# Single first images on ScalarE, the value chain in parts of two and six blocks, the low passes bank by bank, and half a query inside the last product

## What is computed

```python
keys    = xf @ Wk.T                     # (32, 1024, 16)
values  = bn(xf @ Wv.T, per position)   # (32, 1024, 32)
queries = bn(xf @ Wq.T, per k)          # (32, 16, 1024, 4)
content_lambda   = einsum('bmk,bmv->bkv', softmax(keys, axis=1), values)
position_lambdas = einsum('nmk,bmv->bnkv', E, values)     # E is (1024, 1024, 16)
out = x + einsum('bknh,bkv->bhvn', queries, content_lambda)
        + einsum('bknh,bnkv->bhvn', queries, position_lambdas)
```

## Time and profile before

| | |
|---|---|
| median of three runs | 1455.75 us (1455.48 to 1455.85) |
| the profiled execution's own time | 1455.59 us |
| its span | 1453.5 us |
| PE busy | 1426.0 us (98%) |
| DVE, ACT, POOL busy | 852.9 (59%), 752.2 (52%), 421.5 us (29%) |
| mean granted TensorE clock | 0.997 |

### The profile page before, as it was taken

One profiled execution on the slowest core, in us unless ns is written; L12 is line 12 of the kernel. 1 busy time (PEld: TensorE's weight loads), 2 busy tenths in 40 slices (PEclk: granted clock), 3 DMA queues, 4 the chain that ended last, 5 costly groups with the idle time before them and its releaser, 6 DMA issues.

```text
span 1453.5 us, 36061 instructions
## 1 busy us (share of the span) xinstructions
PE 1426.0 (98%) x14551; PEld 1187.9 (82%) x14551; DVE 852.9 (59%) x1217; ACT 752.2 (52%) x1104; POOL 421.5 (29%) x360
## 2 busy tenths in 40 slices
PE   6989999999999999999999999999999999999998
PEld 6987878888888888888888888888888888888886
DVE  7998665555555555555555555555555555555553
ACT  4775465554555455455554555545555454545542
POOL 6683131233223321233223321333123322332120
PEclk9999999999999999999999999999999999999999
DMA  8744413434252333424252333425252233425221
GB/s 290 278 167 90 100 37 87 94 77 84 62 123 65 84 74 87 94 70 89 65 123 65 75 78 93 94 62 97 65 123 65 66 85 94 94 53 105 65 58 29
DMA packets 342618, 134.65 MB, mean 93 GB/s; under 512 B 206800, under 2 KB 337984, under 8 KB 342080
## 3 DMA queue, kind: packets, MB, share of 16 engines
q1 hardware_dynamic: 342592, 134.31, 38.7%
HBM read 109.12 MB, written 25.17 MB: 92 GB/s over the span
## 4 chain that ended last, share of the span: by engine, by line
PE 90%; DVE 0%; issue 0%; DVEq 0%
PE ps_a L1142 81%; PE ps_b L1158 5%; PE ps_a L1126 3%; PE ps_b L1099 0%; DVE lam_diag L864 0%; DVE pos L840 0%; DVE pos L832 0%; DVE res L850 0%; PE ps_b L1107 0%; DVEq L837 0%; DVEq L723 0%
## 5 line engine op out<-in xcount | busy, mean ns | idle before, releaser
L1142 PE MATMUL ps_a<-v_hi,e_hi 128*128 128x512 f32 x1708 | 670.4, 393 | 1.0 <-issue 1.0
L1142 PE MATMUL ps_a<-v_hi,e_lo 128*128 128x512 f32 x1708 | 664.7, 389 | 0.0
L626 ACT ACTIVATE q_diag<-q_blk,q_shift_n,q_scale_n 128x256 f32<-128x256 f32 x512 | 411.4, 868 | 43.7 <-PE ps_b L1158 41.6
L562 ACT ACTIVATE e_hi<-e_nat 128x512 fp32r<-128x512 f32 x305 | 192.8, 633 | 443.2 <-PE ps_a L1142 436.7
L1142 PE MATMUL ps_a<-b_lo,e_hi 128*128 128x512 f32 x976 | 379.6, 389 | 0.0
L1142 PEld LDWEIGHTS ps_a<-v_hi,e_hi 128*128 128x128 f32 x1708 | 320.5, 188 | 68.8 <-issue 1.4
L1142 PEld LDWEIGHTS ps_a<-v_hi,e_lo 128*128 128x128 f32 x1708 | 320.7, 188 | 64.9
L474 POOL TENSOR_TENSOR e_nat<-e_nat,s_buf 128x512 f32<-128x512 f32 x61 | 79.7, 1306 | 927.8 <-DVE e_lo L717 927.8
L807 DVE TENSOR_TENSOR pos<-ps_a,content 128x512 f32<-128x512 f32 x183 | 126.6, 692 | 295.7 <-PE ps_a L1142 295.7
L717 DVE TENSOR_TENSOR e_lo<-e_nat,e_hi 128x512 fp32r<-128x512 f32 x305 | 290.6, 953 | 3.6 <-ACT e_hi L562 3.3
L1142 PE MATMUL ps_a<-t_lo,e_hi 128*128 128x512 f32 x732 | 285.5, 390 | 0.0
(11 more groups left out here) (126 smaller groups left out, 875.8 us busy)
## 6 DMA issues: line engine op xcount, KB each, us to landing
e_nat<-in_L_conv_E SPq DMA_DIRECT2D x128, 512.0 KB, 4.9
res<-in_x SPq DMA_DIRECT2D x64, 256.0 KB, 6.0
out_dram<-res SPq DMA_DIRECT2D x60, 256.0 KB, 4.7
x_main<-in_x SPq DMA_DIRECT2D x24, 512.0 KB, 4.5
q_dram<-q_nat SPq DMA_DIRECT2D x4, 2048.0 KB, 7.6
q_blk<-q_dram SPq DMA_DIRECT2D x32, 256.0 KB, 3.0
x_more<-in_x SPq DMA_DIRECT2D x8, 512.0 KB, 8.6
out_dram<-res SPq DMA_DIRECT2D x4, 192.0 KB, 4.0
```

The costliest lines, as they stand in the source:

```text
L562: nc.scalar.activation(e_hi[:, i], e_source(i, slot), ACT.Copy).then_inc(e_hi_ready, 1)
L626: ins = nc.scalar.activation(to[:, n], of, ACT.Identity, bias=q_shift_n[:, n:n + 1], scale=q_scale_n[:, n:n + 1])
L1142: ins = nc.tensor.matmul(BANK_OF[i], e[:, i, j].rearrange("p n k -> p (n k)"), v[:, j], start=(STARTS[i] and j == 0 and n == 0), stop=(STO ...
```

## The change

- The first batches of images are now 1, 1, 2, 2, 2 images, then four each. The images of the first three batches (0 to 3) are normalised by ScalarE (norm_image) instead of GpSimd, which ends at the bias for them. VectorE's statistics of the first batches are interleaved by half images with gn_finish. TensorE projects image 1 ahead of the transposes of image 2, and averages at the places of AVERAGE_AT.
- TensorE gets dummy transposes of the identity (warm): 12 ahead of the first average, 4 and 7 after it, 30 after the last projection.
- The value chain is in parts of blocks 0 to 1 and 2 to 7 (V_PARTS); affine(0) stands behind the statistics of the second part and ahead of its aggregation. ScalarE splits block 0 in two halves, and TensorE starts with the banks of the first half. keys_max(3) stays behind affine(1).
- first_hi(0, 2) and (0, 3) on ScalarE and first_lo(2) on GpSimd come earlier. sum_keys(2) waits for key_max_ready, not for keys_shifted. e_sums of pair 3 waits for q_affine.
- The banks of the plain pairs go in the order a, c, d, b. spread_content stands ahead of the second half of the low passes, which go bank by bank; lam_scale stands between value_split_lo(4) and (6).
- add_out(2) and evacuate_u2(3) stand ahead of split_lo(3, 6) and (4, 0).
- The last pair is taken out of TensorE's loop; its last product is cut in two, with the left half of its query between them; the additions and stores of its output go by halves.

```diff
-    BATCHES = [(0, GB // 2), (GB // 2, GB // 2)] + [(b, GB) for b in range(GB, B, GB)]
+    BATCHES = [(0, 1), (1, 1), (2, 2), (4, 2), (6, 2)] + [(b, GB) for b in range(2 * GB, B, GB)]
+    ACT_NORMED, ACT_BATCHES = 4, 3
+    V_PARTS = (range(0, 2), range(2, J))
...
@@ GpSimd
+                ins = pool.tensor_tensor(gn_bias[:, sl], gn_out[:, sl, 1], gn_rstd[:, sl], ALU.mult)
+                if k < ACT_BATCHES:
+                    ins.then_inc(gn_biased, 1)
+                    return
...
             first_lo(1)
+            first_lo(2)
             sum_keys(1)
             shift_keys(2)
-            first_lo(2)
             first_lo(3)
             values_rstd(0)
             values_rstd(1)
-            pool.wait_ge(keys_shifted, A)
+            pool.wait_ge(key_max_ready, A)
             sum_keys(2)
             sum_keys(3)
             queries_rstd()
+            pool.wait_ge(q_affine, 1)
             e_sums(PLAIN, PLAIN % 2, 64, first=True)
...
@@ ScalarE
+            def norm_image(b, k):
+                act.wait_ge(gn_biased, k + 1)
+                xi = x_in(b)
+                nc.scalar.activation(xi, xi, ACT.Identity, bias=gn_bias[:, b:b + 1], scale=gn_rstd[:, b:b + 1]
+                                     ).then_inc(x_normed_act, 1)
+            norm_image(0, 0)
+            norm_image(1, 1)
...
                     read_xt(8 * a + i, i, a == 0)
+                    if (a, i) == (A - 1, G - 1):
+                        first_hi(0, 3)
+                    if (a, i) == (0, 1):
+                        norm_image(2, 2)
+                        norm_image(3, 2)
...
             act.wait_ge(v_affine, 1)
-            for j in range(MJ):
-                values_hi(j)
+            first_values_hi(0)
+            first_values_hi(1)
+            values_hi(1)
+            act.wait_ge(v_affine, 2)
+            values_hi(2)
+            values_hi(3)
             normalise(3)
             normalise(2)
             exp_keys(3)
-            act.wait_ge(v_affine, 2)
...
@@ VectorE
+            for part, js in enumerate(V_PARTS):
                 link(value_stats(A - 1, A, range(G - 2, G), js))
+                if part == 1:
+                    affine(0)
                 for j in js:
                     ins = nc.vector.bn_aggr(v_mv[:, j], v_stats[:, j].rearrange("p a s -> p (a s)"))
...
+            affine(1)
...
-            for i in (4, 6):
-                value_split_lo(i)
+            value_split_lo(4)
             lam_scale()
+            value_split_lo(6)
...
             split_lo(PLAIN, 5, PLAIN % 2)
+            add_out(PLAIN - 1, new_block=False)
+            evacuate_u2(PLAIN)
...
+            add_half(PAIRS - 1, 0)
             evacuate_c12(PAIRS - 1)
-            add_out(PAIRS - 1, new_block=False)
+            add_half(PAIRS - 1, 1)
...
@@ TensorE
+            def warm(count):
+                for n in range(count):
+                    nc.tensor.transpose(ps_a[:, 1, 0:P], ident[:], ident[:])
             pe.wait_ge(consts, 6)
+            warm(12)
...
             gn_average(0, 0)
+            pe.wait_ge(weights_loaded, 16 * 3)
+            nc.tensor.transpose(ps_a[:, 0, 0:PC], w_rows[:], ident[0:PC, 0:PC]).then_inc(w_transposed, 1)
+            warm(4)
             pe.wait_ge(gn_read, 1)
             gn_average(1, 0)
             pe.wait_ge(w_ready, 1)
+            warm(7)
+            AVERAGE_AT = {1: 3, 3: 4}
+            for k in range(5, len(BATCHES)):
+                AVERAGE_AT[4 * (k - 5) + 5] = k
...
             project(B - 1, G - 1)
+            warm(30)
...
             for j in range(MJ):
+                if j == 0:
+                    pe.wait_ge(v_hi_first, 1)
+                    plain_sums(0, j, (0, 1), only=(0, 1))
                 pe.wait_ge(v_hi_ready, j + 1)
-                plain_sums(0, j, (0, 1))
+                plain_sums(0, j, (0, 1), only=(2, 3) if j == 0 else None)
...
-            pe.wait_ge(v_lo_ready, 4)
-            for j in range(MJ, J):
-                if j == J - 3:
-                    spread_content()
-                plain_sums(0, j, (2,), last=(j == J - 1))
+            spread_content()
+            for at in range(4):
+                pe.wait_ge(v_lo_ready, (3, 3, 4, 4)[at])
+                for j in range(MJ, J):
+                    plain_sums(0, j, (2,), last=(j == J - 1), only=(at,))
...
-            with pe.Fori(PLAIN + 1, PAIRS) as p:
+            with pe.Fori(PLAIN + 1, PAIRS - 1) as p:
                 pair(p)
-            query(PAIRS - 1)
+            product(PAIRS - 1, 0, False)
+            query(PAIRS - 2)
+            for i in range(1, NP - 1):
+                product(PAIRS - 1, i, False)
+            product(PAIRS - 1, NP - 1, False, range(0, MJ // 2))
+            query_half(PAIRS - 1, 0)
+            product(PAIRS - 1, NP - 1, False, range(MJ // 2, MJ))
+            query_half(PAIRS - 1, 1)
```

More of the change, by code:

```diff
@@ L442, in sum_keys, with values_rstd @@
                 pool.tensor_tensor(of_a, level[:, 0], level[:, 1], ALU.add).then_inc(exp_summed, 1)
-            def values_rstd(half):
-                js = slice(half * MJ, half * MJ + MJ)
-                pool.wait_ge(v_var_ready, half + 1)
+            def values_rstd(part):
+                js = slice(V_PARTS[part].start, V_PARTS[part].stop)
+                pool.wait_ge(v_var_ready, part + 1)
                 pool.tensor_tensor(v_rstd[:, js], v_var[:, js], minus_half[:, js], ALU.pow).then_inc(v_rstd_ready, 1)
@@ L760, in group @@
                 keys_max(a)
-            for k in range(4):
-                gn_moments(k)
-                gn_finish(k)
-            gn_moments(4)
+            gn_moments(0)
+            gn_moments(1, halves=range(0, 1))
+            gn_finish(0)
+            gn_moments(1, halves=range(1, 2))
+            gn_moments(2, range(0, 1), range(0, 1))
+            gn_finish(1)
+            gn_moments(2, range(0, 1), range(1, 2))
+            gn_moments(2, range(1, 2))
+            gn_moments(3, range(0, 1))
+            gn_finish(2)
+            gn_moments(3, range(1, 2))
+            gn_moments(4, range(0, 1))
+            gn_finish(3)
+            gn_moments(4, range(1, 2))
             gn_moments(5, range(0, 2))
@@ L834, in evacuate_first @@
             def evacuate_first(p):
-                for n, (bank, t, cols) in enumerate(((bank_a, 0, left), (bank_d, 1, right), (bank_c, 1, left),
+                for n, (bank, t, cols) in enumerate(((bank_a, 0, left), (bank_c, 1, left), (bank_d, 1, right),
                                                      (bank_b, 0, right))):
@@ L891, in _, with affine @@
             value_stats(A - 1, A - 1, range(G - 2))
-            for half in range(2):
-                js = range(half * MJ, half * MJ + MJ)
+            def affine(part):
+                js = slice(V_PARTS[part].start, V_PARTS[part].stop)
+                dve.wait_ge(params_loaded, 16 * (2 + 2 * TN))
+                dve.wait_ge(v_rstd_ready, part + 1)
+                link(nc.vector.tensor_tensor(v_scale[:, js], v_rstd[:, js], gam_v[:, js], ALU.mult))
+                link(nc.vector.tensor_tensor(v_tmp[:, js], v_mv[:, js, 0], v_scale[:, js], ALU.mult))
+                nc.vector.tensor_tensor(v_shift[:, js], bet_v[:, js], v_tmp[:, js], ALU.subtract).then_inc(v_affine, 1)
+            for part, js in enumerate(V_PARTS):
                 link(value_stats(A - 1, A, range(G - 2, G), js))
+                if part == 1:
+                    affine(0)
                 for j in js:
@@ L980, in pair @@
                     split_lo(p + 1, 0, (i + 1) % 2)
-                add_out(p - 1, new_block=(i == 1))
-                evacuate_u2(p)
+                if not second:
+                    add_out(p - 1, new_block=(i == 1))
+                    evacuate_u2(p)
                 if not last:
@@ L1111, in _, with plain_sums @@
             EVACUATED_BEFORE = (-1, 1, 0, 2, -2, 3, 4)
-            def plain_sums(p, j, passes, last=False):
+            def plain_sums(p, j, passes, last=False, only=None):
                 half, slots_of = j // MJ, FIRST_SLOTS[p]
-                for at, (tile, col, bank) in enumerate(((0, 0, bank_a), (1, 1, bank_d), (1, 0, bank_c), (0, 1, bank_b))):
+                for at, (tile, col, bank) in enumerate(((0, 0, bank_a), (1, 0, bank_c), (1, 1, bank_d), (0, 1, bank_b))):
+                    if only is not None and at not in only:
+                        continue
                     hi = v_hi[:, (0, 4)[half] + col, j % MJ]
@@ L1131, in plain_sums, with product @@
                 return ins
-            def product(p, i, first):
+            def product(p, i, first, js=range(MJ)):
                 pe.wait_ge(e_lo_ready, p * NP + i + 1)
@@ L1139, in product @@
                 hi, lo = value_hi(i), value_lo(i)
-                for j in range(MJ):
+                for j in js:
                     for n, (e, v) in enumerate(((e_hi, hi), (e_lo, hi), (e_hi, lo))):
```

110 lines of the change are left out of this document (70 added, 40 removed).

## The result

The changed kernel takes 1446.65 us (median of 4 runs, 1445.76 to 1447.59) where the kernel before, run beside it, takes 1455.80 (1455.48 to 1456.25): a ratio of 0.9935, 95% interval 0.9923 to 0.9948. Forecast was 1448.3, or 7.45 us less than before; measured are 9.15. Two later series, on chips 12 and 11, gave 9.13 and 8.71.

The account below looks back on a forecast made before the run. The pair loop runs without waits, so only TensorE's standstills and slow stretches elsewhere can be won: 1455.59 - 2.7 (first images) - 3.4 (handover) - 1.0 (pair 3) - 0.3 (end) = 1448.2, against the median 1448.3; range 1446.6 to 1451.2.

Parts of the forecast that it names:

- The start: First images: with one image in the first batch, transposes start earlier; -2.7 us, between -1.2 and -3.3.
- the gain is carried on: Rest of the first stage: TensorE's longest wait is 0.3 us and other engines follow its averages, so -2.7 us stays.
- The handover: From images to products: earlier turn 1.3, three waits gone 2.5, less 0.4; -3.4 us, between -1.6 and -3.9.
- The turn: turn_key_max, behind the first eight matmuls, waits for keys_max and moves from 113.45 to 112.1: -1.3 us.
- Rival 1: Clock falls again while TensorE waits 2.2 us for key_max; eight slow matmuls cost 1.6 us: 1449.9, chance 0.17.
- rival 2: Pair 2's tile load or the first diagonal query is late; only 1.3 of 3.4 us stays: 1450.4, chance 0.10.
- The three waits: TensorE's waits for the values' low part, lam_diag, and the content and first bank all go: 2.5 us, counted by starts.
- The 0.4 against sum_keys(2): Handover: sum_keys(2)'s new place holds one VectorE instruction once; spread up to 1.2 us late, 0.4 of it costing time.
- Pair 3: Fourth product's 1.00 us wait at 204.59 goes as the evacuation moves ahead: -1.0 us, or nothing if VectorE isn't free.
- The end: Last query, addition and stores: half the addition saved, perhaps some issues; -0.3 us, between +0.3 and -0.9.
- rival 5: Behind pair 3 the loop falls into another rhythm, each of 59 pairs waiting; at 0.2 us a pair 1460, chance 0.02.
- Rivals 3 and 4: ScalarE's four normalisations bound the first images, 1449.8, chance 0.07; VectorE bounds the handover, 1453.4, chance 0.03.

Follow-up runs that it names:

- the kernel with pair 3 alone: The kernel before with only add_out and evacuate_u2 of pair 3 moved ahead of the loop's three steps: median 1455.15 us, 1.25 us less, ratio 0.9992.

## Why the prediction was right or wrong

The sign, the places and their order held; the gain is 1.7 us larger than the sum. 1446.65 is just above the low end of the range, 1446.6; the ratio of 0.9935, taken of the 1455.75 on which the range stands, gives 1446.3, below it. The two later series, with 9.13 and 8.71, lie at its low end and inside it.

The 1.7 us have two parts. 0.55 come from the stages, 8.00 between the profiled executions for 7.45: less at the start (0.8), more in the handover (0.25), pair 3 (0.25), the loop (0.2) and the end with its stores (0.6). That the sum of the stages came so near is in part luck, as terms wrong by up to 0.8 us cancelled. The other 1.15, the larger part, stand in no stage. **The step that failed most is the last one of the sum:** it was made on one profiled execution and carried to the median with 0.16 us, as if both kernels' executions stood to their medians alike, and the range left no room for it. The profiled execution was 0.21 below the median in the kernel before, and 0.94 above it in the changed kernel.

**The start** was right as far as it was costed: image 0 at 9.8 (10.2 said), image 4 at 21.57 (21.6 said), -3.0 for -2.7. The step that failed here is the sentence that the gain is carried on through the rest of the stage. first_lo(2) moved ahead of sum_keys(1), and of that move I costed nothing, though I asked for the queue of every step moved. It held key_diag and gave back 1.1 us; undoing the move won it back. This made the gain smaller, not larger.

**The handover**: -3.4 said, -3.65 between the two profiled executions; the total was near, but of its parts only the turn was. The turn: I said that it moves by 1.3 us beyond the start's shift; it came 1.6 earlier against the last projections (11.34 for 12.93), because the clock stayed up and key_max was as early as said. Rival 1 was wrong: at 1.00 through the wait of 1.63 us. The first query, rival 2, was hidden with 1.4 to spare, and without the wait for q_affine TensorE waited 0.8 for it. The three waits all went; undone they cost 1.7, as much as their rows in the kernel before add up to, so my 2.5 from starts was too high for that part. 1.6 and 1.7 leave some 0.3 of the 3.65 that no experiment places. The 0.4 against sum_keys(2) was the wrong kind of term: held were key_diag (1.00) and a normalise (1.35), more than the one instruction I took, but as much is saved later and VectorE has slack in between; its new place is neutral in the medians and wins 0.3 in the traces. The Trainium skill, GPSIMD Engine Reference, section Key points, says that GpSimd shares its SBUF interfaces with VectorE and that they contend, and the trace agrees (key_diag 2.21 and 1.00 for 0.29, v_scale 1.16 for 0.17). The sum that I had made from it, a handover of 2.6 us only, was wrong, since the held steps had slack behind them.

**What made the gain larger than both the sum and the profiled difference** is this standing of the profiled execution to the median. Of the kernel before I had one trace. In two others, with the same code up to there, the clock falls later (between 108 and 110 instead of 106 and 107) and comes back later, and more matmuls are slow (windows of the kernel before, then of the kernel with pair 3 alone; PEclk is the third number from the end):

```profile
114.00:116.00 2.00, 2.00 (x11) 1.69 (x10) 1.25 (x4) 1.69 (x2) 0.00 (x0) 1.00 1.01 159
```

```profile
114.00:116.00 2.00, 2.00 (x6) 1.60 (x6) 1.30 (x3) 1.85 (x2) 0.00 (x0) 0.52 1.13 179
```

Eight matmuls at the low clock there, thirteen here, and a stage of 66.0 against 67.1 us. The changed kernel has no slow stretch there, so against such executions it gains 4.7 in the handover instead of 3.65. On the other side the three profiled executions of the changed kernel are each the slowest of their series, 0.94, 1.90 and 0.39 us above the median, and executions of it draw the hold of key_diag (2.2, or 1.02, which costs nothing: 1.1 us) and the length of the loop (0.8 us). The sizes would do for the 1.15 us. That these draws make it is argued from traces of other executions and not shown for the unprofiled ones, of which only the mean granted clock is on record. In the kernel before this clock points the same way: over five series, 11 executions at 0.996 have a median of 1456.75, 44 at 0.997 one of 1456.26, and the two at 0.998 took 1455.41 and 1455.85. With pair 3's new order alone it does not: seven at 0.996 have a median of 1454.87, four at 0.997 one of 1455.50. So the cause of the 1.15 us stays open.

**Pair 3**: -1.0 said; by the stages -1.25 in the changed kernel, -1.28 alone and -1.36 undone. The term was mis-sized by reading the row's 1.00 us of idle time as the whole, where the handover had been counted by starts.

**The end**: -0.3 said for the addition. The addition saved nothing at all (20.72 for 20.58: two more turns between products and queries eat it), and -1.07 came from the stores, the term that I left at "perhaps some of the issues". In four traces its worth goes with where the packet of the instruction queue falls: ahead of the stores or among the first half of them the last four issues take 2.18 and 1.92 us, among them 3.42 and 2.81. That the packet is the cause is argued; no run moved it alone.

**The loop** fell into no other rhythm (rival 5): 20.51 us a pair as before. Rivals 3 and 4 did not come.

## What to carry to other kernels

When a step is moved within GpSimd's queue, look not only at what waits for it but at which short VectorE instruction on a critical chain now meets two GpSimd instructions back to back: the place of one step of 1.2 us decided 1.1 us of the stage here. A wait of TensorE that ends last has, a fraction behind it, the next: taking away 1.6 us at key_max won nothing until the contention that it moved was taken away too. And one profiled execution is a draw: read two or three of the kernel before, above all in stretches where the clock changes, before a sum is compared with a median.

## What the runs showed of the hardware

- A VectorE instruction of 0.29 us took 1.02 or 2.21 us beside GpSimd: it ended each time within 0.1 us of the end of a GpSimd instruction, the first or the second behind its start. The same code did one in two executions and the other in nine. VectorE's batch statistics were not held beside GpSimd: six took 2.05 us beside the subtraction of 2.38, ten 3.34.
- It goes the other way too: a GpSimd addition of 0.74 us took 7.28 beside three long VectorE subtractions, which then kept their 2.27 us; where GpSimd was served, the same subtractions took up to 3.38.
- The granted clock rose again after as few as 8 or as many as 13 slow matmuls in executions of the same code; it had fallen some 2.4 us later where 13 were slow.
- Four store issues took 2.18 or 3.42 us of SyncE's time, the longer where the packet of the instruction queue lay at the first two: the second issue took 1.82 us instead of 0.56.
